# Row-tiled attention products read their stationary operand 128 columns wide instead of 87

## What is computed

```python
attn = jnp.einsum('bqhd,bkhd->bhqk', q, k)      # q scaled by 16 ** -0.5
attn = jax.nn.softmax(attn, axis=-1)            # 87 x 87 per head, 16 heads
out = jnp.einsum('bhqk,bkhd->bqhd', attn, v)
```

## Time and profile before

| | |
|---|---|
| median of 3 runs | 739.92 us (738.27 to 743.48) |
| span of the profiled execution | 734.0 us (the profile gives no other time of that execution) |
| outside the span, if that execution was a median one | 5.9 us |
| PE busy | 673.9 us (92%) |
| PE loads (PEld) busy | 564.8 us (77%) |
| DVE, ACT, POOL busy | 531.2, 432.0, 491.0 us |
| mean granted TensorE clock | 0.967 |

### The profile page before, as it was taken

The page is one execution under the profiler, slowest core; times in us unless marked ns, Lnnn a source line. Parts: engine busy times, 40 slices in busy tenths (PEclk is TensorE's granted clock), DMA queues, the critical chain, the costliest instruction groups (busy, mean ns, idle before and its releaser), DMA issues.

```text
span 734.0 us, 24407 instructions
## 1 busy us (share of the span) xinstructions
PE 673.9 (92%) x9431; PEld 564.8 (77%) x9431; DVE 531.2 (72%) x1192; ACT 432.0 (59%) x1115; POOL 491.0 (67%) x564
## 2 busy tenths in 40 slices
PE   5998998999985799999999999999999999999873
PEld 3987887888853577888888888888888888887652
DVE  2468687887978646788878878878878887866642
ACT  4553452635442346677777676677776777776541
POOL 3667563764648428787877877876976977975442
PEclk9999999999996969999999999999999999999996
DMA  8963472231011223223232332332332332122001
GB/s 222 237 163 116 129 224 47 54 83 44 22 24 40 59 54 79 63 70 82 67 78 73 75 83 73 79 82 72 78 83 68 79 86 67 42 54 62 26 25 34
DMA packets 69528, 58.73 MB, mean 80 GB/s; under 512 B 30607, under 2 KB 68646, under 8 KB 69286
## 3 DMA queue, kind: packets, MB, share of 16 engines
q1 hardware_dynamic: 69414, 57.18, 30.9%
HBM read 33.69 MB, written 11.40 MB: 61 GB/s over the span
## 4 chain that ended last, share of the span: by engine, by line
PE 71%; DVE 12%; issue 4%; ACT 4%; SPq 3%; POOL 3%; DMA 2%; POOLq 0%; DVEq 0%; ACTq 0%
PE p_a L1355 13%; PE p_c L1355 10%; PE p_conv L758 8%; PE p_kv L758 7%; PE p_o L1427 6%; PE p_s L1415 5%; PE p_mm L758 4%; PE p_s L1397 4%; PE p_n L1435 3%; PE p_c L1474 3%; PE p_a L1381 3%; PE p_s L1411 2%; DVE t L1282 2%; DMA kr<-qkT 2%; DVE kv L656 1%
## 5 line engine op out<-in xcount | busy, mean ns | idle before, releaser
L1291 DVE TENSOR_REDUCE mx<-p_s 87x16 bf16<-87x1392 f32 x64 | 102.5, 1602 | 44.6 <-PE p_s L1397 44.4
L1214 ACT ACTIVATE prT<-p_s 87x1392 f32<-87x1392 f32 x64 | 85.2, 1331 | 29.3 <-PE p_s L1415 27.8
L1121 POOL TENSOR_TENSOR t<-t,ss_rs 116x512 f32<-116x512 f32 x48 | 50.9, 1060 | 58.9 <-ACT ss_rs L1190 57.8
L426 POOL TENSOR_TENSOR xs_lo<-xcols,xs_hi 120x585 fp32r<-120x585 f32 (+1 forms) x45 | 60.4, 1348 | 43.7 <-ACT xs_hi L483 43.7
L1415 PE MATMUL p_s<-qr,kr 32*87 32x87 f32 x2048 | 68.8, 257 | 0.0
L1115 POOL TENSOR_TENSOR t<-t 116x512 f32<-116x512 f32 x48 | 62.4, 1299 | 5.6 <-DVE t L1282 5.6
L1135 POOL TENSOR_TENSOR yT_lo<-y_raw,yT_hi 128x232 fp32r<-128x232 f32 x48 | 32.5, 678 | 47.1 <-issue 31.4
L1124 POOL TENSOR_TENSOR t<-t,tabs 116x512 f32<-116x512 f32 x48 | 61.2, 1276 | 2.7
L1415 PEld LDWEIGHTS p_s<-qr,kr 32*87 32x87 f32 x2048 | 60.3, 154 | 0.0
L1411 PE MATMUL p_s<-mxT,pick_row 32*87 32x87 bf16 x1024 | 55.7, 208 | 1.9 <-ACT mxT L1208 1.9
L1427 PE MATMUL p_o<-prT,vp 87*32 87x87 f32 x2048 | 55.1, 248 | 0.1
(11 more groups left out here) (287 smaller groups left out, 2077.8 us busy)
## 6 DMA issues: line engine op xcount, KB each, us to landing
xcols<-in_x_cols SPq DMA_DIRECT2D x12, 822.7 KB, 8.1
h<-h_tokens SPq DMA_DIRECT2D x16, 348.0 KB
out<-out_sb SPq DMA_DIRECT2D x48, 116.0 KB
h_tokens<-in_txt SPq DMA_DIRECT2D x4, 1232.0 KB, 8.7
x<-in_txt_cols SPq DMA_DIRECT2D x32, 154.0 KB, 4.1
qr<-qkT SPq DMA_DIRECT2D x64, 58.0 KB, 2.0
kr<-qkT SPq DMA_DIRECT2D x64, 58.0 KB, 2.0
vp<-vt SPq DMA_DIRECT2D x32, 87.0 KB
```

Of the source, the lines that this page charges most:

```text
L426: nc.gpsimd.tensor_tensor(xs.lo[:, n % XS_SLOTS, :, 0:M].bitcast(F32R), raw, xs.hi[:, n % XS_SLOTS, :, 0:M], ALU.subtract).then_inc(S['xs_ ...
L1214: nc.scalar.activation(prT[:, k % 2], p_s[0:SEQ, :, 0:QUADS * SEQ], ACT.Exp, scale=HD ** -0.5).then_inc(S['s_exp'], 1)
L1291: nc.vector.reduce_max(mx[:, k % 2, :, 0:QUADS], p_s[0:SEQ, :, 0:QUADS * SP].rearrange("p j (a k) -> p j a k", k=SP)[:, :, :, 0:SEQ], AX_X ...
```

## The change

The first product of `peak`, and both products of `scores`, take 128 columns of the stationary operand and write 128 partitions of `p_s` in place of 87. The 41 partitions more are read by nobody. For the last image of a group that reads past column 347, so the strips grow from 350 to 390 columns (`STRIP`), and `pick_row` from 87 to 128. The larger strips move other tensors in on-chip memory, and POOL waits for the window part's row stores before its first write of `hb`.

```diff
+STRIP = SEQ * (GB - 1) + P + 1
...
-        self.pick_row = sb("pick_row", [P, QUADS, SEQ], BF16)
+        self.pick_row = sb("pick_row", [P, QUADS, P], BF16)
...
             last = nc.gpsimd.affine_select(out=self.pick_row[:], in_=self.pick_row[:], compare_op=ALU.not_equal, fill=1.0,
-                                           base=-ROW * j, pattern=[[-1, QUADS], [0, SEQ]], channel_multiplier=1)
+                                           base=-ROW * j, pattern=[[-1, QUADS], [0, P]], channel_multiplier=1)
...
-        qr = sb("qr", [P, 2, QUADS, GT + 2])
-        kr = sb("kr", [P, 2, QUADS, GT + 2])
+        qr = sb("qr", [P, 2, QUADS, STRIP])
+        kr = sb("kr", [P, 2, QUADS, STRIP])
...
                         pool.wait_ge(consts.S['rope_in'], 48)
+                        for part in range(2):
+                            pool.wait_ge(W[f'st_rows{part}'], ROWS_OUT * len(range(part, STEPS, 2)))
...
-                            mm_ = nc.tensor.matmul(p_s[0:SEQ, j, a * SP:(a + 1) * SP], rows(qr, j, a, SEQ).bitcast(F32R),
+                            mm_ = nc.tensor.matmul(p_s[:, j, a * SP:(a + 1) * SP], rows(qr, j, a, P).bitcast(F32R),
...
-                            nc.tensor.matmul(p_s[0:SEQ, j, a * SEQ:(a + 1) * SEQ], pick_row[ROW * j:ROW * (j + 1), a],
+                            nc.tensor.matmul(p_s[:, j, a * SEQ:(a + 1) * SEQ], pick_row[ROW * j:ROW * (j + 1), a],
...
-                            mm_ = nc.tensor.matmul(p_s[0:SEQ, j, a * SEQ:(a + 1) * SEQ], rows(kr, j, a, SEQ),
+                            mm_ = nc.tensor.matmul(p_s[:, j, a * SEQ:(a + 1) * SEQ], rows(kr, j, a, P),
                                                    rows(qr, j, a, SEQ), start=False, stop=True, skip_group_check=True)
```

## The result

The changed kernel takes 765.45 us (median of 4, 761.21 to 770.04) against 740.54 us for the kernel before: the ratio is 1.0367 (95% interval 1.0316 to 1.0419). The forecast was 751.7 us, slower; the sign and the range (729 to 766) hold, the size doesn't: by the medians 24.9 us were lost (the ratio stands for 27.2) where 11.8 were forecast. The profiled execution took 763.17 us with a span of 761.5, 1.7 us outside the span. It is about 1.7 us in every execution that has both on record. If it was so for the kernel before's profiled execution too, that one took about 735.7 us, and most of the 5.9 us counted as outside its span was the distance of a quick execution from the median. The forecast of the difference doesn't change by it.

A forecast was written before the change was run, and what follows sets the result against it. TensorE was taken to bound the group part. Per image +280 (scores), -16 (picks), -60 (peaks) gave +204 ns; times 58 images +11.8 us, so 751.7 us against the median of 739.92, range 729 to 766.

The forecast's parts named there:

- TensorE bounds the group part: Group part: PE busy 27.4 us or more of each 28 us stretch from 300 to 664 us; only partly bounding at both ends.
- Plain float32 loads at 128 columns cost 0.85 ns per column more: Scores block, both passes: 41 more columns cost 35 ns per step, +280 ns per image.
- Picks: fast, but only the first load exposed: Scores block: bf16 load 96 ns against 112; the other three run beside a scores stream of 73 ns; -16 ns per image.
- Between the ends of +35 and -15 per step I take -15: Peak block: F32R loads of 128 columns taken as fast, four steps, -60 ns per image; other end +140.
- the prediction's 58 images: Group part: 64 images with twelve counted half; 58 x 0.204 us gave +11.8 us.
- The first rival: Peak block: F32R loads slow at 128 columns, peaks +140 ns, +404 per image, 763 us; chance 0.25 with or without slow picks.
- Half weight for twelve images: Three of 16 groups, where PE is busy 104 of 135 us and often waits: the per-image cost counted half.
- a pick step has load 73: Scores block: an 87-column picks load set at 73 ns against a stream of about 39, so the load sets the step.
- Strips, fills, wait, layout: 0: Outside the loads: `pick_row` selects at most +1.2 us, strips' clears at most +0.6, POOL's wait and moved tensors 0; taken 0.
- the rule weighed in the prediction: Skill's rule on all touched loads: fast with exactly 128 weights and non-FP32 type; the trace's fast float32 transposes were held against it.

The follow-up runs named there:

- the layout alone: Changed kernel with all stationary operands 87 wide again, long strips, moved tensors and POOL's new wait kept: 741.21 us, ratio 0.9994 to the kernel before.
- picks alone wide: Kernel before with only the picks' stationary operand (`pick_row`) widened to 128 columns, strips and layout as before: 740.77 us, ratio 0.9978.
- the bf16 peaks: Long-strip kernel with all operands 87 wide, peaks reading the upper half of each float32 as bf16: at 87 wide 731.24 and 728.78 us, at 128 wide 728.65 us.
- picks ahead at 87: All 16 picks of a block issued ahead of its scores, everything 87 wide, against the kernel before: 735.43 us, ratio 0.9937.

## Why the prediction was wrong in size

1. *TensorE bounds the group part.* Right: +388 ns per image in its blocks, +24.9 us in the time, and PE full in the steady stretches.
2. *Plain float32 loads at 128 columns cost 0.85 ns per column more, and both passes pay it.* Right: 264 ns were forecast for the scores block with the picks' gain, 251 measured.
3. *Picks: fast, but only the first load exposed.* Right in sign and place: -23 ns alone against -16.
4. *"Between the ends of +35 and -15 per step I take -15, because F32R is, like a transpose, a single pass, and bf16 is fast too."* This is the step that failed. F32R loads take 189 ns at 128 columns, on the line of plain float32: +137 ns per image where -60 was in the sum. At the prediction's 58 images these 197 ns are 11.4 us, the bulk of the miss of 13.1; the rest is within the noise. The first rival (763 us) had it, from rows that carried the right type at two widths; the transposes that outweighed them share neither type of product nor purpose. A number of passes is no measure of how weights load.
5. *Half weight for twelve images.* Neither shown nor refuted. With the measured 388 ns the full count gives 24.8 us and the half weight 22.5, both within the noise of the 24.9. That the full count fits is in part luck, as the profiled executions show: the first period grew by 6.7 us in place of 1.55, with the clock low for longer, and the 13 periods after the second by 1.21 each on the mean in place of 1.55, 15.7 us in place of 20.2.
6. *"a pick step has load 73".* Wrong without consequence here, and the most useful miss: the rate per column was fitted on float32 loads and applied to bf16. It made the pick steps look bound by their load when they waited behind a float32 stream, and so hid the gain of another order.
7. *Strips, fills, wait, layout: 0.* Right, by the layout alone.

On the rule weighed in the prediction: the Trainium skill, TensorE: Matmul & The Clock Gate, section "Weight-path perf modes — Fast Weight Load (FWL) and DoubleRow", wants 128 weights and a type other than FP32. With F32R counted as FP32, as the profile prints it, all three touched loads follow it: bf16 at 128 columns takes 95 ns (picks alone wide) against 112 to 117, both float32 kinds 189 to 191. The source pattern that the packed trace keeps for each load agrees: the 128-wide bf16 ones are read as 32 x 4 elements, the F32R and plain float32 ones as 128 in one run. So are the float32 transposes of 128 columns in the kernel before; whatever makes them short, it isn't that read, and this could be seen before any run. The 87-wide bf16 loads are one run as well, and most of the gain of the bf16 peaks came with them, 135 of 162 ns.

What stays open: whether the longer stretch at 1.2 GHz near 260 us belongs to the change. Picks 128 and picks ahead at 87 have shorter blocks than the kernel before and yet a longer such stretch, and each kernel has one profile to read. Single executions of the kernel before differ by some us too, with the granted clock: over 25 of them the longest span is 746.6 us at a mean clock of 0.950, the shortest 734.2 at 0.966. No run held the clock fixed. And why a float32 transpose loads 128 columns in 141 ns and 87 in 155 was not tried.

## What to carry to other kernels

Before widening a stationary operand for a faster load, look for a load of that very type and width in the trace; neither the same element size nor the same number of passes stands in for it. Where loads set the step, write down for each step the longer of its own stream and the next load: order and element type can then be worth more than width: here 233 ns per image and 17 us (a part of it the clock's) without a single column more. Here a slow load behind a short stream was exposed, and a faster one behind a long stream gained nothing, so the short steps belonged side by side. And compare the granted clock of the executions before a time is put down to the blocks.

## What was not expected of the hardware

- A bf16 load of 87 columns in a row tile lets the next step follow after about 44 ns, a float32 or F32R load of 87 columns after 77; that is at most about 0.5 ns per column (the stream may set it) against 0.83.
- The same float32 strips, read as bf16 at a distance of four bytes, load as fast as packed bf16 (95 ns at 128 columns, for 94 to 96 of the picks).
- A matmul block behind which an ordinary product follows also ends sooner with bf16: from the last step's start to the next line 189 ns with F32R and 141 with bf16, both at 87 columns.
- The clock accounts for most of the spread between executions of one kernel: 0.35 us more of span for each us at 1.2 GHz, over 25 executions.
